# The queries' inverse root mean square, from GpSimd's power to Newton steps on VectorE

## The reference, cut to what matters

```python
def rmsnorm(x, w, eps=1e-06):
    return x * jax.lax.rsqrt(jnp.mean(x * x, axis=-1, keepdims=True) + eps) * w
q = (h @ Wq_c @ Wq_up).reshape(b, t, H, D).transpose(0, 2, 1, 3)
q = rmsnorm(apply_partial_rope(q, cos, sin), q_norm_w)
k_sw = rmsnorm(apply_partial_rope(h @ Wk, cos, sin), k_norm_w)
...
sw_scores = jnp.einsum('bhtd,bsd->bhts', q, k_sw) * scale
sw_scores = CAP * jnp.tanh(sw_scores / CAP)
...
sw_out = attend(sw_scores, sw_mask[None, None], sink, v_sw, 'bhts,bsd->bhtd')
```

## Time and profile before

| | us |
|---|---|
| runs | 600.37, 593.98, 595.01 |
| median | 595.01 |
| the profiled execution's own time | 597.21 |
| its span (first to last instruction) | 595.4 |
| mean granted TensorE clock, share of full | 0.98 |

### The profile page before, as it was taken

How to read it: one execution, slowest core, us unless ns; L and a number is a source line. 1 busy time by engine, 2 the same in 40 slices (tenths; PEclk the granted TensorE clock), 3 DMA queues, 4 the chain that set the end, 5 groups by cost and what they waited for, 6 DMA issues and landing times.

```text
span 595.4 us, 9656 instructions
## 1 busy us (share of the span) xinstructions
PE 522.0 (88%) x2951; PEld 397.9 (67%) x2951; DVE 334.4 (56%) x884; ACT 312.5 (52%) x739; POOL 328.9 (55%) x235
## 2 busy tenths in 40 slices
PE   0998988799777899999999999999988898899981
PEld 0655776588566678778787777988856444465561
DVE  3389832314056282652935629343356898999643
ACT  1215126365464776757757577575632238666530
POOL 3000438868677586685866858854312024888860
PEclk9999999899797999999999999999999999999997
DMA  9940629887886986675675756866368102556667
GB/s 289 375 149 6 165 66 216 183 173 187 209 240 155 251 215 150 128 169 112 145 175 127 169 117 142 187 147 142 35 171 264 52 21 78 81 88 98 97 80 220
DMA packets 87281, 90.39 MB, mean 152 GB/s; under 512 B 26688, under 2 KB 75264, under 8 KB 86848
## 3 DMA queue, kind: packets, MB, share of 16 engines
q1 hardware_dynamic: 66608, 61.50, 36.1%
q0 software_dynamic: 19584, 27.24, 27.5%
q10 hardware_dynamic: 1040, 1.05, 0.5%
HBM read 65.32 MB, written 22.60 MB: 148 GB/s over the span
## 4 chain that ended last, share of the span: by engine, by line
PE 40%; DVE 18%; issue 15%; DMA 9%; ACT 9%; POOL 8%; SPq 0%; POOLq 0%; ACTq 0%; DVEq 0%
PE bank L559 8%; DMA expert_sums<-expert_weights,token_of_slot 7%; PE bank L896 6%; PE bank L904 3%; PE bank L905 3%; PE bank L551 2%; PE bank L523 2%; POOL tiles L1098 2%; PE bank L1804 2%; DVE sum_squares L686 2%; ACT normed L607 2%; POOL expert_sums L866 2%; POOL expert_weights L858 2%; POOL expert_sums L1105 2%; PE bank L491 2%
## 5 line engine op out<-in xcount | busy, mean ns | idle before, releaser
L866 POOL DMA_INDIRECT expert_sums<-expert_weights,token_of_slot x79 | 131.1, 1659 | 57.1 <-ACT expert_weights L928 39.4
L858 POOL DMA_INDIRECT expert_weights<-normed_x,token_of_slot x79 | 92.2, 1167 | 111.5 <-DVE token_of_slot L366 47.2
L896 PE MATMUL bank<-expert_weights 128*88 128x128 f32 x632 | 84.2, 276 | 1.3 <-ACT expert_weights L921 1.2
L896 PEld LDWEIGHTS bank<-expert_weights 128*88 128x88 f32 x632 | 74.6, 159 | 2.1 <-issue 2.1
L559 PE MATMUL bank<-out_weights,expert_weights 128*128 128x256 f32 x256 | 60.1, 380 | 1.4 <-ACT expert_weights L644 1.4
L928 ACT ACTIVATE expert_weights<-bank,chosen_bf 128x256 f32<-128x256 f32 x79 | 37.7, 478 | 36.4 <-issue 22.2
L904 PE MATMUL bank<-expert_weights 88*128 88x256 f32 x158 | 48.4, 388 | 6.9 <-ACT expert_weights L928 5.7
L1105 POOL DMA_INDIRECT expert_sums<-expert_weights,token_of_slot x23 | 46.3, 2011 | 14.5 <-issue 5.5
L559 PEld LDWEIGHTS bank<-out_weights,expert_weights 128*128 128x128 f32 x256 | 46.4, 190 | 8.2 <-ACT expert_weights L644 3.1
L719 DVE SCALAR_TENSOR_TENSOR expert_weights<-bank,blocks_valid 128x64 f32<-128x64 f32 x32 | 7.1, 221 | 75.6 <-ACT expert_weights L621 68.7
L905 PE MATMUL bank<-expert_weights 89*128 89x256 f32 x158 | 48.1, 385 | 0.0
(11 more groups left out here) (272 smaller groups left out, 1084.7 us busy)
## 6 DMA issues: line engine op xcount, KB each, us to landing
expert_weights<-experts_out SPq DMA_DIRECT2D x79, 192.8 KB
expert_weights<-experts_in SPq DMA_DIRECT2D x79, 176.0 KB
expert_weights<-L_ffn_wi SPq DMA_DIRECT2D x32, 128.0 KB
expert_weights<-w_comp SPq DMA_DIRECT2D x1, 2048.0 KB, 9.2
expert_weights<-fold_g SPq DMA_DIRECT2D x1, 2048.0 KB, 13.4
expert_sums<-zeros SPq DMA_DIRECT2D x2, 1024.0 KB, 17.9
expert_weights<-L_ffn_wo SPq DMA_DIRECT2D x16, 128.0 KB
normed<-expert_sums SPq DMA_DIRECT2D x2, 1024.0 KB, 5.6
```

Source lines behind the costliest of these rows:

```text
L858: nc.gpsimd.indirect_dma_start(xt0[g % 4], None, xn0, bass.IndirectOffsetOnAxis(ap=MAP[:, g:g + 1], axis=0)).then_inc(gathered[g % 4], 16)
L866: nc.gpsimd.indirect_dma_start(sums0[g % 2], bass.IndirectOffsetOnAxis(ap=MAP[:, g:g + 1], axis=0), yt0[g % 2], None, compute_op=ALU.add). ...
L896: ins = nc.tensor.matmul(ps[5][0:DHB, c * P:(c + 1) * P], w[:, k * DH + c * DHB:k * DH + (c + 1) * DHB], xT0[g % NXT][:, k * P:(k + 1) * P ...
```

## The change

The power on GpSimd is taken out together with `power_at`. In `query_rms`, which takes the place of `query_mean`, VectorE forms the inverse root itself: after the mean (L677 of the changed kernel) the bits of the number, read as an integer, are scaled by -0.5 and added to a constant, which gives a first guess; three Newton steps of three operations each follow. All are of 128x16 elements, all but the last are linked, and the semaphore `qpow`, for which `query_norm` waits, is now raised by VectorE.

```diff
+        RTMP = sb("rms_steps", 2 * H)
...
-        def query_power(pool, t):
-
-            r = RR[:, t % TPB * H:(t % TPB + 1) * H]
-            pool.wait_ge(qss, t + 1)
-            nc.gpsimd.tensor_tensor(r, r, MHALF[:, 0:H], ALU.pow).then_inc(qpow, 1)
...
-        def query_mean(st, t):
-            j = t % TPB
+        def query_rms(dve, st, t):
+
+            x = RR[:, t % TPB * H:(t % TPB + 1) * H]
+            y, a = RTMP[:, 0:H], RTMP[:, H:]
             st.wait()
-            nc.vector.tensor_scalar(RR[:, j * H:(j + 1) * H], SSQ[:, j * H:(j + 1) * H], 1.0 / D, RMS_EPS, ALU.mult, ALU.add).then_inc(qss, 1)
+            nc.vector.tensor_scalar(x, SSQ[:, t % TPB * H:(t % TPB + 1) * H], 1.0 / D, RMS_EPS, ALU.mult, ALU.add).then_inc(qss, 1)
+            dve.wait_ge(qss, t + 1)
+            st.link(nc.vector.tensor_scalar(y.bitcast(I32), x.bitcast(I32), -0.5, float(0x5f3759df), ALU.mult, ALU.add))
+            for i in range(3):
+                st.link(nc.vector.tensor_tensor(a, y, y, ALU.mult))
+                st.link(nc.vector.scalar_tensor_tensor(out=a, in0=a, scalar=-0.5, in1=x, op0=ALU.mult, op1=ALU.mult))
+                if i < 2:
+                    st.link(nc.vector.scalar_tensor_tensor(out=y, in0=a, scalar=1.5, in1=y, op0=ALU.add, op1=ALU.mult))
+            nc.vector.scalar_tensor_tensor(out=x, in0=a, scalar=1.5, in1=y, op0=ALU.add, op1=ALU.mult).then_inc(qpow, 1)
...
-            query_mean(st, t)
+            query_rms(dve, st, t)
...
-                power_at = {beats(g, NG)[0]: g + 1 for g in range(FIRST_STEP, NT - 1)}
...
-                    if i in power_at:
-                        query_power(pool, power_at[i])
```

## The result

| kernel | runs, us | median |
|---|---|---|
| before | 600.37, 593.98, 595.01, 594.78 | 594.89 |
| changed | 614.03, 614.15, 611.13, 615.11 | 614.09 |

The change makes the kernel slower: ratio 1.0285, 95% interval 1.0246 to 1.0324, or 17 us on 595. The forecast was 604.5 us with a range from 594.5 to 612.5. The direction and the mechanism are as forecast. The size is not well hit: by the ratio, 595.0 x 1.0285 = 612.0 us lies 0.5 inside the range's upper end, the median of 614.1 lies outside it, and both lie outside the 599 to 611 that the prediction gave to its own case. The profiled execution took 614.03 us (span 612.2), 16.8 more than that of before.

The account below looks back on a forecast made before the run. TensorE was taken as nearly the bound, in steps 2 to 6 waiting almost only for VectorE's L719. Terms -4.2 - 5.0 + 2.1 + 10.3 + 6.3 = +9.5 us on 595.0 gave 604.5 us, range 594.5 to 612.5.

Parts of the forecast that it names:

- its own case: The forecast's main case, 604.5 us with its own range of 599 to 611; chance 0.50.
- What bounds: Steps 2 to 6: TensorE nearly the bound, waiting almost only for VectorE's L719, five times, 4.6 us in all.
- The links: VectorE before the gate: ten chained starts at 0.205 us add 2.05 us per tile; +10.3 us in steps 2 to 6, +2.1 in step 1.
- The split of the wait: TensorE's scores, steps 2 to 6: 0.33 us of the delay falls at s = 2, the wait at s = 3 becomes 2.66.
- The clock: TensorE, steps 2 to 6: clock falls behind the longer waits, three falls in five steps at 2.1 us, +6.3 us.
- What GpSimd gives back: Earlier scatters shorten TensorE's early waits: -4.2 us in step -1, -5.0 us in step 1, 0 in steps 2 to 6.
- The wait at 193.04: TensorE's wait of 2.17 us after the third power, with five beats between: no change, 0.
- That the clock holds: Rival: a wait of 2.66 us does not lower TensorE's clock; +3.2, 598.2 us; chance 0.27.
- The smaller price: Rival: VectorE's links at the pace of unlinked operations, -4.4 us; 590.6 us; chance 0.10 shared with the larger return.
- the larger return: Rival: both GpSimd returns in full, 11.8 us, no clock fall; +0.6, 595.6 us; chance 0.10 shared with the smaller price.
- A return that reaches further: Rival: GpSimd runs ahead through steps 1 and 2, the wait at 193.04 goes too; 588.7 us, chance 0.08.
- The fourth rival: TensorE's clock falls in every full step and GpSimd's returns are half; +22.3, 617 us; chance 0.05.

Follow-up runs that it names:

- e3_late_newton: Changed kernel with guess and Newton steps moved behind the second half's window norm, right before the query norm: 591.09 us, ratio 0.985 to the kernel before.
- e5: The changed kernel itself, timed again in the second group: 613.61 us, ratio 1.032 to the kernel before.
- e10: The changed kernel itself, timed again in the third group: 612.89 us, ratio 1.025 to the kernel before.
- The filler: Changed kernel plus eight unread 128x256 matmuls on TensorE ahead of the last scores of steps 2 to 6: 605.81 us, ratio 1.012 to the kernel before.
- e7_one_step: Changed kernel with one Newton step instead of three, four added instructions instead of ten: 603.84 us, ratio 1.012 to the kernel before.

## Why the prediction was right, and where its sizes were off

- **What bounds.** Right: in steps 2 to 6 the only wait of note was that for L719 of s = 2, and all that is put in front of it comes out at its end. e3_late_newton shows it by moving nothing but the place.
- **The links.** 2.05 us per tile forecast, 2.2 measured; six tiles make 13.2 instead of 12.4 us. Most of the difference is the first start: the guess stands 0.34 us behind the mean where 0.205 was taken. From the table for SBUF to SBUF in the Trainium skill ("VectorE: DVE Perf Modes", section on the TRN2 errata) the prediction had estimated 77 ns per operation; L681 takes 175 ns, so the trace disagrees. The same section has (N + 151) cycles at 0.96 GHz for a float32 tensor_tensor, checked there at N = 512 and 2048; an estimate from it for N = 16 is 174 ns, and with this the trace agrees.
- **The split of the wait.** 0.33 and 2.66 forecast, 0.34 and 2.58 measured. Nothing behind them gave anything back.
- **The clock.** The mechanism was right, the term mis-sized: +6.3 us (three falls in five steps at 2.1) against five falls in five steps. By the ledger they cost 42.8 - 37.5 - 2.2 = 3.1 in step 2 to 3, then 1.6, 1.7 and 1.6, and 0.6 at the last, 8.6 in all. (The last fall costs 1.6 too: at the first scores of step 7, 405.58 against 387.77, the changed kernel is 17.8 us behind; 1.0 of that is made up by the end of the span.) The first costs more because the clock stays low for longer behind it: 0.50 from 217 to 220 us and 0.55 from 220 to 223. Two more profiles of the changed kernel (e5 and e10) have four and five falls in these steps, one of 3.2 and 3.0 us and the others of 1.6 to 1.9, so the prediction had too few falls, and its 2.1 for one was near the mean. The filler shows that it is the clock: with the wait filled, the term is gone.
- **What GpSimd gives back.** Forecast 9.2, measured 6.3 by the ledger, 5.1 by the mean of fourteen profiles, 6.9 and 5.3 as the difference of medians in the kernels without powers. In step -1 the ledger has 3.7 (4.2 forecast). In step 1 it was 2.6 where I had 5.0: of the terms this is the one that failed most. I had named the pace of gather and scatter, 3.2 us per beat, but took too little for it: from 143.68 us on GpSimd issues them one behind the other with gaps of 0.30 us, and at 150.84 TensorE waits 2.58 us, where it waited 1.86 with the powers, and the clock falls there again (L486 in 1.97). The prediction also put that wait of 1.86 down to an output copy. By the earlier trace rows it ended with L612, a copy of transposed queries; this one stands in ScalarE's queue right behind an output copy (L928 at 154.99, L612 at 155.36), so the argument is not touched.
- **The wait at 193.04.** Forecast unchanged, 0; in the ledger it grew from 2.17 to 3.61 at 190.47, +1.4 us. But this is not a cost of the change: in the two other profiles of the changed kernel it is 1.48 and 2.44 us, and in the two kernels without powers and Newton steps 2.51 and 1.41. It varies from one execution to the next. That a scatter which lands late sets it is read from the trace only; no run was made for it.
- **The sum** of the measured terms: -6.3 + 13.2 + 8.6 + 1.4 = +16.9, beside the 16.8 between the two profiled executions. Forecast: +9.5. The four sizes that were off (0.8 for the links, 2.3 for the clock, 2.9 for what GpSimd gives back, 1.4 for the wait) all err to the same side and make 7.4 us. So the direction is no luck: the links, the largest term, came out nearly as forecast. That the time by the ratio still falls into the range, by 0.5 us, is luck.
- **The rivals.** That the clock holds is refuted (0.95 over the full steps, five falls). The smaller price is refuted by the links (0.205 us and more apart), the larger return, 11.8 us, by both kernels without powers (at most 10.8 by the interval of the first, 6.9 by that of the second). A return that reaches further, 18 us, is refuted by the same. The fourth rival, 617 us with a chance of 0.05, came nearer to the measured time than the forecast did: its first half, a fall in every full step, happened, at 1.6 to 3.1 us each where that rival had 2.9; its second half, a return of 4.6, did not quite (5 to 7). That case deserved a larger chance.

## What to carry to other kernels

An operation moved off an engine saves nothing in the steps where that engine ends no wait; what it costs depends on what stands behind it in its new queue. Look for the engine whose queue ends the bound engine's wait, and put new work behind the last instruction that the bound engine waits for: here the same ten instructions made 591 us at one place and 613 at the other. A wait on TensorE costs more than its length once the clock falls behind it, so shortening it can pay twice. And a term of 1 or 2 us that is read off two single executions may be what varies between executions: a second profile of the same kernel tells.

## What the runs showed of the hardware that was not expected

- Whether the clock of TensorE falls behind a wait is not a matter of the wait's length alone: it fell behind 1.66, 1.96 and 2.08 us and held behind 1.86 in one kernel (e7_one_step); in the kernel before it held behind 2.17 at 193.04. What else decides was not tested.
- A float32 matmul of 128x256 counts as two instructions in the profile and took 0.43 us (16 in 3.45), so eight of them were twice the filler I meant. With them TensorE did 3.45 us more work per step, and the kernel was still 8 to 12 us faster than without, by the ratios.
